# Routed experts of an AdaLN block: 88 dense weight slots against 111 gathered token blocks

## The reference

```python
shared_out = _silu_and_mul(xf @ shared_w1.T) @ shared_w2.T          # hidden 352
logits = xf @ gate_w.T                                              # 16 experts
probs = jax.nn.softmax(logits, axis=-1)
routing_weights, selected = jax.lax.top_k(probs, 6)
combine = zeros((T, E)).at[arange(T)[:, None], selected].add(routing_weights)
gate_up = jnp.einsum('th,eoh->teo', xf, w1)                         # 16 experts, 2 * 176 rows
act = _silu_and_mul(gate_up)
moe_out = jnp.einsum('te,tei,ehi->th', combine, act, w2)
x = x + gb * (moe_out + shared_out)
```

## Time and profile before

| | before |
|---|---|
| median of 3 runs | 583.57 us (581.69 to 585.34) |
| the profiled execution | 582.13 us |
| its span, first to last instruction | 580.0 us |
| mean granted TensorE clock | 0.985 |
| PE busy | 94% of the span |
| DVE busy | 76% |
| POOL busy | 51% |
| ACT busy | 43% |
| DMA | 71 GB/s over the span |

### The profile page before, as it was taken

The page is one execution under the profiler, slowest core; times in us unless marked ns, Lnnn a source line. Parts: engine busy times, 40 slices in busy tenths (PEclk is TensorE's granted clock), DMA queues, the critical chain, the costliest instruction groups (busy, mean ns, idle before and its releaser), DMA issues.

```text
span 580.0 us, 7523 instructions
## 1 busy us (share of the span) xinstructions
PE 544.6 (94%) x2492; PEld 434.2 (75%) x2492; DVE 438.0 (76%) x827; ACT 252.0 (43%) x485; POOL 293.4 (51%) x226
## 2 busy tenths in 40 slices
PE   6998898999989999998989889998999999999996
PEld 4677686777878778876867668886777878887884
DVE  4588586896868865788877875598987877787784
ACT  1433444434444455344434454544354455544542
POOL 0125225745656354456755534466656546656650
PEclk8998998999999999999999999999998999999999
DMA  8904003114341100103210301111311111113111
GB/s 287 385 10 173 0 4 103 44 36 122 100 137 64 37 12 27 53 19 122 78 55 18 102 1 35 40 37 37 110 55 37 57 38 64 63 37 126 57 37 36
DMA packets 22526, 41.41 MB, mean 71 GB/s; under 512 B 3732, under 2 KB 8856, under 8 KB 22104
## 3 DMA queue, kind: packets, MB, share of 16 engines
q1 hardware_dynamic: 22216, 40.93, 21.6%
q10 hardware_dynamic: 272, 0.00, 0.0%
HBM read 38.69 MB, written 2.23 MB: 71 GB/s over the span
## 4 chain that ended last, share of the span: by engine, by line
PE 40%; DVE 34%; issue 9%; ACT 7%; POOL 6%; DMA 3%; SPq 0%; DVEq 0%; ACTq 0%; POOLq 0%
PE gate_ps L461 11%; PE up_ps L461 10%; PE sum_ps L633 9%; PE pre L461 6%; DVE hidden L1028 5%; DVE down_lo L1011 4%; DVE act_lo L1031 4%; DVE hidden L1017 4%; ACT act_hi L740 3%; DVE ln_t L790 2%; POOL hidden L1100 2%; POOL up_lo L1093 2%; DVE stats L862 2%; ACT up_hi L725 2%; DVE ln_y L794 1%
## 5 line engine op out<-in xcount | busy, mean ns | idle before, releaser
L1093 POOL TENSOR_TENSOR up_lo<-w_slots,up_hi 128x512 fp32r<-128x512 f32 x100 | 135.2, 1352 | 94.0 <-ACT up_hi L725 94.0
L1100 POOL TENSOR_TENSOR hidden<-hidden,routing_rows 128x512 f32<-128x512 f32 x88 | 113.9, 1295 | 110.7 <-DVE hidden L1017 82.0
L740 ACT CAST act_hi<-hidden 128x512 fp32r<-128x512 f32 x100 | 62.1, 621 | 224.9 <-DVE hidden L1028 217.0
L1011 DVE TENSOR_TENSOR down_lo<-w_slots,down_hi 128x256 fp32r<-128x256 f32 x100 | 98.0, 980 | 38.5 <-ACT down_hi L728 35.2
L1031 DVE TENSOR_TENSOR act_lo<-hidden,act_hi 128x512 fp32r<-128x512 f32 x100 | 78.1, 781 | 60.4 <-ACT act_hi L740 60.4
L461 PE MATMUL gate_ps<-h_hi,up_hi 128*128 128x512 f32 x200 | 82.9, 414 | 9.5 <-POOL up_lo L1093 8.9
L461 PE MATMUL up_ps<-h_hi,up_hi 128*128 128x512 f32 x200 | 81.1, 405 | 0.8 <-DVE hidden L1028 0.8
L633 PE MATMUL sum_ps<-act_hi,down_hi 128*128 128x512 f32 x200 | 79.0, 395 | 1.2 <-DVE act_lo L1031 0.7
L461 PE MATMUL up_ps<-h_lo,up_hi 128*128 128x512 f32 x200 | 80.2, 401 | 0.0
L461 PE MATMUL gate_ps<-h_hi,up_lo 128*128 128x512 f32 x200 | 80.1, 400 | 0.0
L461 PE MATMUL up_ps<-h_hi,up_lo 128*128 128x512 f32 x200 | 80.0, 400 | 0.0
(11 more groups left out here) (156 smaller groups left out, 763.1 us busy)
## 6 DMA issues: line engine op xcount, KB each, us to landing
routing_rows<-routing_dram SPq DMA_DIRECT2D x32, 256.0 KB, 3.3
routing_rows<-routing_dram SPq DMA_DIRECT2D x16, 224.0 KB, 2.8
routing_rows<-routing_dram SPq DMA_DIRECT2D x16, 192.0 KB, 2.8
w_slots<-routed_w SPq DMA_DIRECT2D x1, 2688.0 KB, 18.5
routing_rows<-routing_dram SPq DMA_DIRECT2D x16, 160.0 KB, 2.8
w_slots<-routed_w SPq DMA_DIRECT2D x1, 2304.0 KB, 9.2
x_rows<-x SPq DMA_DIRECT2D x4, 512.0 KB, 3.7
routing_rows<-routing_dram SPq DMA_DIRECT2D x16, 128.0 KB, 2.8
```

The costliest lines, as they stand in the source:

```text
L740: e.copy(act_hi[g % 2][:, :], hidden[g % 3][:, :]).then_inc(act_hi_done, 1)
L1011: e.tensor_tensor(down_lo[ring][:, :], w_slots[:, s, UP_COLS:SLOT_COLS], down_hi[ring][:, :].bitcast(F32), ALU.subtract).then_inc(down_lo_ ...
L1093: e.tensor_tensor(up_lo[g % 2][:, :], w_slots[:, slot_of(g), 0:UP_COLS], up_hi[g % 2][:, :].bitcast(F32), ALU.subtract).then_inc(up_lo_don ...
L1100: e.tensor_tensor(hidden[g % 3][:, :], hidden[g % 3][:, :], routing_rows[ring][:, :], ALU.mult).then_inc(routed_done, 1)
```

## The change

Preparation and routing are now done for all four batches first, in ticks: batch b starts 14 ticks after batch b-1, each batch has 31 steps (`batch_steps`). The second norm is written token by token into `payload`, whose rows hold 256 features, the token's number and the 16 probabilities (276 floats). `rank` counts each token's place within the region of each of its six experts, and `scatter` sends every row to its six places in `xs` in DRAM by 24 indirect DMAs a batch of 128 rows each, issued from POOL. The shared expert stays dense (12 slots over 512 tokens) and runs inside the ticks.

`table` then works out for each of `BLOCKS` = (2048 x 6 + 16 x 127) // 128 = 111 blocks of 128 rows its expert and its first row. Regions are padded with rows that add to rows nobody reads. The routed part is a loop over the 111 blocks, in which the expert's weights are addressed by a register. Weights of all 16 experts, split, stay in SBUF; four experts are prepared in the ticks, three behind them, nine during the first nine blocks.

The diff's core:

```diff
+BLOCKS = (TOKENS * TOP_K + EXPERTS * (P - 1)) // P
+REG_GROUP = 14
+BLK_RING = 6
+Y_RING = 4
+ACCS = 3
+BATCH_TICKS = 14
@@ schedule @@
+    for tick in range(5, ticks):
+        for b in range(BATCH):
+            step = tick - BATCH_TICKS * b
+            if 0 <= step < len(steps[b]):
+                order += steps[b][step]
@@ sync: after the ticks @@
+            for i in range(BLOCKS):
...
+                if i >= BLK_RING:
+                    e.wait_ge(added[(i - BLK_RING) % ACCS], added_by(i - BLK_RING))
+                row = e.snap(regs[i // REG_GROUP % 2][i % REG_GROUP], min_val=0, max_val=DUMMY_ROW)
+                e.dma_start(blk[i % BLK_RING][:, :], xs[bass.ds(row, P), :]).then_inc(blk_in[i % BLK_RING], 16)
+                if late:
+                    for stage, at in late.pop(0):
+                        stages[stage](at)
...
+            def load_sums(b):
+                for k in range(ACCS):
+                    e.dma_start(acc_rows[b % 2][k][:, :, :], accs[k][b * SEQ:(b + 1) * SEQ, :]...)
@@ tensor @@
+            for i in range(BLOCKS + 3):
+                if i < BLOCKS:
+                    turn_block(i)
+                if 0 <= i - 1 < BLOCKS:
+                    up_block(i - 1)
+                if 0 <= i - 2 < BLOCKS:
+                    turn_act(i - 2)
+                if i - 3 >= 0:
+                    down_block(i - 3)
@@ scalar @@
+            for i in range(BLOCKS + 3):
+                    split_block(i)      # h_t_hi  <- h_t_ps   128x256
+                    tanh_block(i - 1)   # block_act <- both_ps 128x176
+                    split_act(i - 2)    # act_t_hi <- act_t_ps 88x256
+                    take_y(i - 3)       # y_rows  <- y_ps     128x256
@@ vector @@
+            for i in range(BLOCKS + 2):
+                    split_block(i)
+                    weigh_block(i)
+                    act_block(i - 1)
+                    split_act(i - 2)
@@ gpsimd @@
+            def scatter(b, t):
+                for n in range(TOP_K):
+                    e.indirect_dma_start(xs, bass.IndirectOffsetOnAxis(ap=place_at[b % 2][:, t, n:n + 1], axis=0),
+                                         payload[b % 2][:, t, :], None).then_inc(scattered[b % 2], 16)
...
+            for i in range(BLOCKS):
+                e.wait_ge(y_done, i + 1)
+                e.wait_ge(blk_in[i % BLK_RING], 16 * (i // BLK_RING + 1))
+                if i >= ACCS:
+                    e.wait_ge(added[i % ACCS], added_by(i - ACCS))
+                e.indirect_dma_start(accs[i % ACCS], bass.IndirectOffsetOnAxis(
+                    ap=blk[i % BLK_RING][:, ID_COL:ID_COL + 1].bitcast(I32), axis=0), y_rows[i % Y_RING][:, :], None,
+                    compute_op=ALU.add).then_inc(added[i % ACCS], 16)
```

More of the change, by code:

```diff
@@ L105, in part_of_slot @@
-def part_of_slot(s):
-    return next(i for i, (a, b) in enumerate(W_PARTS) if a <= s < b)
-def prepare_steps(b):
-    def norm(p):
-        return [[("stats", b, p)], [], [("normed", b, p)], [("turn", b, p)], [("split", b, p)]]
-    widen = [("widen_gain", b)] if b >= 1 else []
-    return norm(0) + [
-        widen + [("input_gates", b, 0)],
+TOKENS = BATCH * SEQ
+REGION = TOKENS + P
+DUMMY_ROW = EXPERTS * REGION
+XS_ROWS = DUMMY_ROW + P
+ID_COL = DIM
+PROB_COL = DIM + 1
+ROW_COLS = DIM + 1 + PADDED + 1
@@ new lines, in down_pieces, with pieces_through, batch_steps @@
+def down_pieces(e):
+    pieces = []
+    for half in range(2):
+        at = 0
+        while at < HALF:
+            row = e * EXPERT_HIDDEN + half * HALF + at
+            n = min(HALF - at, P - row % P)
+            pieces.append((half, at, at + n, row // P, row % P))
+            at += n
+    return pieces
+UP_PIECES = up_pieces()
+def pieces_through(e):
+    return sum(piece[0] <= e for piece in UP_PIECES)
+def batch_steps(b):
+    return [
+        [("load_wide", b), ("stats", b, 0)], [], [("normed", b)], [("turn", b, 0)], [("split", b, 0)],
+        [("input_gates", b, 0)],
@@ new lines, in batch_steps, with expert_stages @@
+        [("add_shared", b)]]
+def expert_stages(e):
+    return [("expert_up", n) for n in range(pieces_through(e - 1), pieces_through(e))] + [("expert_down", e)]
+def schedule():
+    steps = [batch_steps(b) for b in range(BATCH)]
+    order = [("stats", 0, 0), ("normed", 0), ("warm_up", WARM_UP), ("combine_weights", 0), ("mods",),
+             ("turn", 0, 0), ("split", 0, 0), ("combine_weights", 1), ("half_bias",)]
+    extra = {6: [("mod_rows",)], 8: [("split_shared", 0)], 9: [("split_shared", 1)], 10: [("split_shared", 2)]}
+    early = [stage for e in range(EARLY_EXPERTS) for stage in expert_stages(e)]
+    for n, stage in enumerate(early):
+        extra.setdefault(16 + 2 * n, []).append(stage)
+    steps[0][:5] = [[], [], [], [], []]
+    ticks = BATCH_TICKS * (BATCH - 1) + len(steps[0])
+    for tick in range(5, ticks):
[3 more added lines that the diff above has]
+                order += steps[b][step]
+                if ("rank", b) in steps[b][step] and b == BATCH - 1:
+                    order.append(("table",))
+        order += extra.pop(tick, [])
+    assert not extra
+    return order
```

1385 lines of the change are left out of this document (839 added, 546 removed).

## The result

| | before | after |
|---|---|---|
| median | 583.66 us of 4 runs (581.69 to 585.34) | 857.76 us of 4 runs (852.75 to 861.27) |
| ratio, with its 95% interval | 1 | 1.469 (1.459 to 1.480) |
| span of the profiled execution | 580.0 us | 859.5 us |
| mean granted TensorE clock | 0.985 | 0.754 |

The change makes the kernel 47% slower. The direction was forecast (692 us, slower 0.82); the size was not: 166 us are missing from the sum, and 858 lies outside the range of 575 to 800.

What follows compares the result with a forecast made beforehand. PE was taken to bound the kernel before; after the change, the ring of block buffers would pace the loop. Ticks 272, blocks 359, filling and drain 23, end 38 summed to 692 us; range 575 to 800.

Steps and rivals of the forecast that it cites:

- What bounds the kernel now, and PE's gain: Routed slots: PE is the bound; 363 us of PE removed, 249 added by blocks, a gain of 114 on PE alone.
- Part 1: Preparation of all batches in ticks, through batch 3's scatters and their landing: 272 us until the block loop.
- I take 5 us a batch as lost (0 to 15): Ticks: delay a batch from scatters on POOL ahead of the next batch's output weights, added to 52 us.
- the 77%: Ticks: DVE's busy share, taken from 20 to 60 us of the old profile; 40 us of work becomes 52 a batch.
- Part 2: Block loop: the ring of six buffers sets the pace, 9.7 us for three rounds, 3.23 a block, 359 us.
- The rival of the lower clock: Block loop: PE falls to the lower clock, 3.8 us a block, 755 us in all; chance 0.20 together with register operations.
- The estimate from the Trainium skill: Block loop: addition 2.3 us instead of 4.0, block 2.67, loop 296 us; not used in the sum.
- Rival 1: Block loop and scatters: cheap DMAs, 2.58 us a block, 575 in all (545 with DVE 90% busy); under 577: chance 0.15.
- Rival 3: Block loop and scatters: slow software DMAs, issue 1.8, landing 6, 4.5 us a block, 890 us in all; chance 0.10.
- Rival 4: Block loop: PE's 8 register operations at 0.2 us make a round 3.8 us; chance 0.20 together with the lower clock.
- Part 3: Filling: experts 7 to 15 in 20 pieces, 41 us where nine blocks take 29, +12; drain behind the last block, +11.
- Part 4: End of the kernel: sums read back, added by DVE and POOL, and stored: 38 us.

Runs made afterwards that it cites:

- ring8: The changed kernel with eight block buffers in the ring instead of six, and a small table moved into a block buffer: 728.3 us.
- both edits: Scatters of batches 0 to 2 spread two a tick, POOL's passes moved to DVE; run with eight buffers and loads three blocks ahead against the changed kernel: 655.3 us.
- fill2: The changed kernel with two identity products on PE ahead of the wait for each block's load: 853.0 us.
- fill4: The changed kernel with four identity products on PE ahead of the wait for each block's load: 841.0 us.
- noacc: The changed kernel with block results written by a plain indirect DMA instead of one that adds to its target: 800.4 us.
- fill: The changed kernel with eight identity products on PE ahead of the wait for each block's load: 882.1 us.
- ring8_reg7: The kernel with eight block buffers, with block numbers loaded into registers every 7 blocks instead of every 14: 720.3 us.

## Why the prediction was right and wrong

**What bounds the kernel now, and PE's gain.** Right. Most rounds in ring8 take 2.12 us, the forecast had 2.24 of PE's own work. The loop at that pace would be 235 us against 363 for the dense slots.

**Part 1, the ticks: the step that failed most, +93 us.** The time of an indirect DMA was right: 1.27 us from one to the next (0.99 and 0.30), 1.2 forecast. What failed is "I take 5 us a batch as lost (0 to 15)". The prediction named the very passes (L1440, ahead of the projection) and then sized their delay by the ticks in which scatters stand, 22 us of issue less 11 us of ticks. But a queue in order does not spread. What PE waited for was L1449, behind all 24 scatters and not 18: it was idle 29 us a batch, nearly the 30 us that its scatters take. Taking the queue away gave 69 us in three batches, 23 each. Of the remaining 24 us, 15 are there at batch 0's first scatter (104.7; the forecast's steps give 90), and 10 in the three periods. All +93 us are there at batch 3's first scatter (333.2, 240 by the forecast); its 24 scatters and their landing took the 32 us forecast. DVE's work was near the 40 us forecast (36.5 in each of the first two periods of the kernel after), but the 77% at which it was to be busy did not carry over to the ticks: 45% in these two periods, and 61 to 70% with both edits.

**Part 2, the ring: the mechanism right, the size short.** Each sign asked for is there: PE under 75%, idle ahead of the turn, released by the load; the load released by the addition; groups of three. 11.1 us instead of 9.7 for a group:

| term | forecast | measured |
|---|---|---|
| round of PE | 2.4 | 3.64, lower clock |
| `take_y` and hand-overs | 0.5 | 0.85 |
| addition, issue to landing | 4.0 | 3.7 |
| load, here with its hand-overs | 2.8 | 2.9 |

The two DMA terms, 6.8 together, were 6.6, though no row showed anything of an addition; the miss of this group is PE's round. The rival of the lower clock had 3.8 us a block and 422 us for the loop; 3.74 was measured. It was set aside: "with such rounds PE would be busy all the time, which brings the clock back". It isn't: only the first round of three runs at the lower clock, and that is the one in the ring. Yet fill2 and fill4 brought the clock to 0.94 and 0.98 and the block only to 3.63. So by the accounts of single groups the lower clock is nearly all of the miss (1.24 of 1.4 us in three blocks), and by taking it away only one fifth (0.11 of 0.51 us a block). Of what takes its place, the longer rounds with loads of registers are 0.09 us a block; the rest stays open. These loads, which the forecast had at nothing (its 2.4 counts the 8 operations), are 0.2 us a block in ring8.

**The addition.** The estimate from the Trainium skill for a DMA issued from GpSimd (DMA: Bandwidth & Descriptors, Anatomy of one DMA), 2.3 us and a block of 2.67, was too low for this one: 3.8 by the page of the kernel after. The plain indirect write in noacc landed after 2.5, near it. Rival 1 needed the addition under 2.5 us; it does not even hold for the write without adding, where the loop still ran at 3.18. Rival 3 needed an issue of 1.8 and a landing of 6: neither. The stated bound on one issue, 0.8 to 1.6 us, held (0.99 and 1.55).

**Rival 4, register operations,** falls by fill and by the rounds of 2.12 us in ring8. Its place is taken, at 0.2 us a block, by the loads of registers, which it did not mean. **Rival 1**'s side remark of 545 us doesn't come out of its terms: 40/0.9 is 44.4 instead of 52, which takes 23 from 575.

**Part 3.** The pieces' 41 us were right (40.8), their being the only pace was not (58.4); +20. **Part 4** was right within 4 us.

**The range** failed because its terms were taken as independent and its top as one bad price. The measured time is three middling misses of one sign, 93, 20 and 50, and two of them, the ticks and the filling, have one cause: queues in order that had been priced by the work in them, not by who stands behind. None of the signs named for a wrong forecast came (a start before 240, under 2.7 us a block, a clock near 0.5, an issue outside 0.8 to 1.6): no sign was set for a late start.

## What to carry to other kernels

Work that an engine issues in a bunch delays what stands behind it by the whole bunch, whatever share of the stage the engine is busy. Price it by the first instruction behind the bunch and who waits for that. An average over many rounds hides stops in a few of them: look at single rounds before calling a cause absent. A ring's pace is its latency over the blocks in flight: one more buffer was worth 90 us with no engine having less to do.

## What the runs showed of the hardware

- An indirect DMA of 128 rows from POOL takes 0.96 us of POOL in the median and 0.99 in the mean (up to 1.40), the next one starts 0.30 us later; with an addition 1.55 us. Landing is 2.5 us after issue (2.4 to 5.2), with an addition 3.8 (3.6 to 5.1).
- A load of 14 values into registers of PE took 1.3 to 1.6 and 3.5 to 3.7 us in turn (ring8), one of 7 values 1.1 to 2.0 (ring8_reg7). PE's products stood still meanwhile (3.45 us before 514.65).
- After 3 us of idle time PE ran a round of 16 small products at the lower clock, 3.64 instead of 2.12 us, and was back at the upper one for the next.
- Sixteen copies of 138 KB beside POOL's scatters landed after 3.3 us each in one run of the kernel after and 11.4 in another, with the same code; it moved the first block by 14.6 us.
- Keeping PE's clock up by products of an identity in float32 costs 0.22 us each: eight a round made the kernel 24 us slower. Four made it 17 us faster in a single run; two gave 853.0 us, which is no gain beyond the spread of the runs.
